# Sorting the tokens by expert inside the attention loop

## The chip, the cores and the metric

One core of a Trainium2 chip runs the whole program. The metric is the device time of one execution in microseconds: the median of three runs. Engines are named as the profile does: PE (matrix products; PEld is its weight loading), DVE (VectorE), ACT (ScalarE), POOL (GpSimd) and SP (SyncE, which issues most transfers).

## What is computed

A cross-attention layer and a mixture of experts, each with a residual:

```python
x = x + xattn(layernorm(x), ctx_1024, cos, sin, ...)      # 8 batches, 512 x 256 rows, 1024 context rows, 16 heads of 64
y = layernorm(x)                                          # the experts' input
shared = gelu(y @ shared_up) @ shared_down                # 256 -> 1024 -> 256
probs = softmax(y @ router_w)                             # 8 experts
top_k_prob, top_k_idx = top_k(probs, 2)
routed = sum(gate[e] * (gelu(y @ routed_up[e]) @ routed_down[e]) for e in the two chosen)
out = x + shared + routed + y
```

The attention's logits are clipped to -11..11 after scaling; all data are float32.

## The kernel before

**Stages.** `prepare` brings in weights and the first batch. `attention` has a loop over seven batches and the eighth one unrolled (`batches`, L543); each batch has eight turns, one for each pair of heads (`slot(b, p)` of every engine, p = 0 to 7, called the first to the eighth turn here). `experts` computes the shared expert for seven batches, then 12 big routed tiles of 512 rows and 15 small ones of 256, and last the shared expert of the eighth batch. Every engine has its program written out in order; semaphores alone tie them together.

**A batch in attention.** In the fifth turn of pass b the attention result of batch b - 1 is normalized: VectorE computes moments, GpSimd the reciprocal root (`rstd`, L693, a power), VectorE `norm_shift` (L1296), ScalarE `normalize` (L1114) from x_out to xn. In the seventh and eighth turns PE transposes xn, and at the end of the eighth computes the router's logits (`route_by_columns`, L865), which ScalarE copies out (`copy_logits`, L1120). SyncE stores xn to `normed` in HBM in the sixth turn (`store_norm`, L558).

**Order in the fifth turn.** GpSimd: the two subtractions of the staged context (`low_stage`, L697), then rstd. VectorE: clip, sums, `multiply_out`, the moments, clips and sums again, then in this order

```python
            clip(4)
            if p == NORMS - 1 or p < NORMS and not last(b):
                norm_shift(p, ...)          # waits for GpSimd's rstd
            add_up(4)
            add_up(5)
```

ScalarE runs the exponentials of scores (L1039) and waits for VectorE's sums before it overwrites one of four probs buffers; at the turn's end it normalizes. PE waits for exponentials (scores) and clips (products with v). SyncE waits for the two subtractions (`store_stage`, L564) before it issues `spread_rden` (L586). In the fourth turn GpSimd has two subtractions of staged x and an rstd. In each turn it also stores a piece of zeros to the sorted rows (L705).

**Routing in the experts.** While the shared expert runs, VectorE takes the logits of all 4096 tokens (32 tiles of 128), finds the two best experts, their gates and the rank of each token among those of its expert (with two matmuls by a triangle and by ones, `rank_rows`), and from the counts the packed start of every expert in units of 256 rows (from L2085 to L2136). Then GpSimd scatters: for each of eight batches it copies four numbers a token beside the row (L1844) and issues eight indirect transfers of 128 rows of 1040 bytes (L1848) to `sorted_rows`, two batches being reloaded to freed buffers on the way (L1853). `s_scatall` then lets SyncE load the first routed rows (L1708). `tables` computes which rows and expert each tile has.

Of the kernel before, what the change touches and what calls it, by code (L numbers as in the profile page):

```python
# [17 lines left out]
P = 128  # L18
ZERO = 325
# [6 lines left out]
class Shapes:  # L26


    def __init__(self, x, ctx, cos, Wq, routed_up):
# [17 lines left out]
        self.DW = self.D + 4  # L47
        assert 2 * self.HD == P and self.KD == 2 and self.N == 512 and self.KT == 8 and self.PAIRS == 8


def prepare(nc, sh, es, mem, x, ctx_in, cos, sin, lat_g, lat_b, ctx_g, ctx_b, Wq, Wkv, Wo, wpack, keep):
# [16 lines left out]
    def sem(name):  # L68
# [8 lines left out]
    AT = dict(k_two=0, k_rope=2048, x_raw=4096, probs=7168, k_two_split=13312, o=15360, o6=18432, x_all=25088, v1=30208,  # L77
              whole=32256, xn_T=33280, den_sb=34304)
# [252 lines left out]
    def scalar_x(act, k):  # L331
# [6 lines left out]
                w_two=w_two, w_five=w_five, k1_two=k1_two, clo=s_clo, lats=s_lats, wvlo=s_wvlo, wout=(s_wout, 48), wo=(s_wo, 16),  # L338
# [3 lines left out]
def attention(nc, sh, es, mem, prep, x, ctx_in, bo, router_w, wpack, ctxT, latT, start, xn_d, xnT, xs, den_d, rden_d, keep):  # L342
# [93 lines left out]
    def result_norm(b):  # L436
# [17 lines left out]
    x_all = sb("x_all", [P, 3, QT, D])  # L454
    x_in, x_out, xn = (x_all[:, i] for i in range(3))
# [9 lines left out]
                 v0=KT * 2 * P, probs=PROBS * 2 * N, k_split=4 * S, o=PAIRS * N, q_all=5 * N, sums=6 * N, x_all=3 * QT * D,  # L465
# [6 lines left out]
    n_var, n_rstd, n_shift = ([sb(f"n_{what}{i}", [P, QT]) for i in range(NORMS)] for what in ("var", "rstd", "shift"))  # L472
    rw = sb("rw", [P, KD, E])
    bo_bc = sb("bo_bc", [P, D])

# [47 lines left out]

    def batches(eng, slot):

        with nc.Fori(0, LAST, engines=[eng.engine], hint_back_edge=True) as b:
            for p in range(PAIRS):
                slot(b, p)
        for p in range(PAIRS):
            slot(LAST, p)  # L530

    def sync(sp, shared_weights, first_rows):
# [19 lines left out]
        sp.sem_inc(s_xnout, 16)  # L552
# [5 lines left out]
        def store_norm(to, n, normed):  # L558
            sp.wait_ge(s_normed, normed)
            sp.dma_start(xn_d[to].rearrange("(p t) d -> p t d", p=P), xn).then_inc(s_xnout, 16)  # L560
# [47 lines left out]
        def slot(b, p):  # L608
# [18 lines left out]
            if p == PAIRS - 3:  # L627
# [5 lines left out]
                store_norm((b + (B - 1)) % B, b + 1, result_norm(b))  # L633
# [36 lines left out]
    def gpsimd(pool):  # L670
        flat = xs.rearrange("r d -> (r d)").rearrange("(c p z) -> c p z", p=P, z=ZERO)
        PARTS = flat.shape[0] // B
        assert PARTS * B == flat.shape[0] and PARTS <= PAIRS
        prep["gpsimd"](pool)
        pool.memset(neg_half[:], -0.5)
        pool.memset(p_sum[1], 1.0)
# [13 lines left out]
        pool.memset(x_out, 0.0).then_inc(s_zeroed, 1)  # L690
# [11 lines left out]

        def slot(b, p):
            if p < PARTS:
                pool.dma_start(flat[b * PARTS + p], keep["zero"][:]).then_inc(s_zero, 16)  # L705
# [6 lines left out]
            elif p < NORMS:  # L712
                rstd(p, b * NORMS + (p + 1))

# [5 lines left out]
        def zeroed():  # L720
            pool.wait_ge(s_zero, 16 * flat.shape[0])
# [3 lines left out]
    def tensor(pe):  # L725
# [150 lines left out]

        def weigh_tile(p, j):
# [6 lines left out]
        def slot(b, p):  # L884
# [44 lines left out]
            def weigh_two(j):  # L929
                pe.wait_ge(s_clip, b * (PAIRS * STEPS) + (G + j + 4))  # L930
                if j == 0:
# [3 lines left out]
                    if p == 0:  # L935
                        pe.wait_ge(s_lgout, b + 1)
                for t in (j, j + 1):
# [49 lines left out]
            if p == PAIRS - 1:  # L987
                pe.wait_ge(s_dencp, b * PAIRS + (p + 2))
                route_by_columns(act_before(b, p, nth(b, p, "t", 1) + 1), sum_ps[:, before_p % 2])
            weigh_two(2)  # L990
# [41 lines left out]
    def scalar(act, split_weights):  # L1032
        act.sem_inc(s_exp, 2)
        act.sem_inc(s_u, 1)
# [85 lines left out]
        def copy_logits(to, n, src):  # L1120
            act.wait_ge(s_lg, n)
            act.activation(logits[:, bass.ds(to * QT, QT)], src[:, 0:QT * E].rearrange("p (t e) -> p t e", e=E),
# [5 lines left out]
        def slot(b, p):  # L1128
# [63 lines left out]
            if p == PAIRS - 1:  # L1192
                copy_logits((b + (B - 1)) % B, b + 1, sum_ps[:, before_p % 2])
# [5 lines left out]
            exps(6, 7)  # L1199
            if p == NORMS - 1 or p < NORMS and not last(b):  # L1200
                if p == NORMS - 1:

                    act.wait_ge(s_xnout, 16 * b + 16)
# [17 lines left out]
        def last_norm():  # L1221
            act.wait_ge(s_xnout, 16 * B + 16)
# [8 lines left out]
        def last_logits():  # L1231
            copy_logits(LAST, B + 1, proj[0])
# [1115 lines left out]
```

## Time and profile before

| | us |
|---|---|
| three runs | 2253.99, 2255.81, 2255.84 |
| median | 2255.81 |
| span of the profiled execution | 2252.6 |

Of the profiled execution the span is what is recorded; the median of the runs is 3.2 us above it. Busy in this execution: PE 2166.5 us (96%), VectorE 1763.5 (78%), ScalarE 1354.5 (60%), GpSimd 419.1 (19%). A busy PE isn't PE at its peak, since ends of matmuls are modelled; an instruction's duration holds the time in which it is held up once it is started. "Issue" as releaser means that the profile shows nothing the engine waited for.

### The profile page before, as it was taken

How to read it: one execution, taken by the hardware profiler on the slowest of the kernel's cores; microseconds unless marked ns; L12 is line 12 of the kernel's file. 1: busy time of each engine (PE TensorE's matmuls, PEld its weight loads, DVE VectorE, ACT ScalarE, POOL GpSimd, SP SyncE). 2: the span in 40 equal slices, each digit the busy share in tenths (PEclk: the TensorE clock that was granted, in tenths of full speed). 3: DMA queues.
4: the chain of work that ended last, by engine and by line, in shares of the span. 5: the costliest groups of instructions: out<-in, count | busy, mean ns of one | idle time of the engine just before them, and what ended most of it. 6: DMA issues, size and time to landing. Idle time of an engine off the chain costs nothing. (4 is left out here: it accounts for less than half of the span.)

```text
span 2252.6 us, 48833 instructions
## 1 busy us (share of the span) xinstructions
PE 2166.5 (96%) x18002; PEld 1591.0 (71%) x18002; DVE 1763.5 (78%) x2342; ACT 1354.5 (60%) x1942; POOL 419.1 (19%) x358
## 2 busy tenths in 40 slices
PE   6999999999999999999999999999639999999999
PEld 5666666666666666666666666648539999999998
DVE  7999899889889899998988988995303565556775
ACT  6675676666567567666656755654114556556775
POOL 2110120111011011011101110004740122223222
PEclk9999999999999999999999999999659999999999
DMA  7344335335334533523533442244542454546773
GB/s 263 91 130 148 89 111 179 89 98 168 107 96 130 154 83 116 177 86 103 171 96 101 147 140 67 59 136 137 195 160 85 136 135 122 140 126 168 224 225 99
DMA packets 154291, 297.77 MB, mean 132 GB/s; under 512 B 34688, under 2 KB 79616, under 8 KB 152064
## 3 DMA queue, kind: packets, MB, share of 16 engines
q1 hardware_dynamic: 136176, 264.60, 38.2%
q0 software_dynamic: 17664, 30.45, 5.8%
q8 instruction: 136, 2.23, 0.4%
q10 hardware_dynamic: 288, 0.26, 0.0%
q14 instruction: 27, 0.22, 0.0%
HBM read 181.44 MB, written 79.72 MB: 116 GB/s over the span
## 5 line engine op out<-in xcount | busy, mean ns | idle before, releaser
L1039 ACT ACTIVATE probs<-scores 128x1024 f32<-128x1024 f32 x512 | 503.6, 1025 | 325.6 <-PE scores L754 312.8
L1345 DVE TENSOR_TENSOR sums<-sums,probs 128x1024 f32<-128x1024 f32 x384 | 470.2, 1225 | 14.2 <-issue 1.7
L880 PE MATMUL sum_ps<-probs,v_nat 128*64 128x512 f32 x2056 | 476.6, 599 | 3.6 <-DVE probs L1244 3.6
L754 PE MATMUL scores<-q_split,k_split 64*128 64x512 f32 x3072 | 415.2, 394 | 1.8 <-ACT probs L1039 1.8
L1244 DVE TENSOR_SCALAR probs<-probs 128x2048 f32<-128x2048 f32 x256 | 314.2, 1227 | 107.8 <-ACT probs L1039 107.4
L1927 PE MATMUL sum_ps<-down,hid_split 128*128 128x256 f32 x2640 | 361.4, 285 | 35.2 <-issue 34.1
L1927 PEld LDWEIGHTS sum_ps<-down,hid_split 128*128 128x128 f32 x2640 | 346.8, 193 | 54.9 <-issue 41.6
L1901 PE MATMUL scores<-xT,up 128*128 128x512 f32 (+1 forms) x1680 | 354.4, 351 | 19.0 <-issue 18.2
L2065 DVE TENSOR_TENSOR hid_split<-hid,hid_split 128x512 fp32r<-128x512 f32 x204 | 141.3, 692 | 252.4 <-ACT hid_split L1991 187.4
L754 PEld LDWEIGHTS scores<-q_split,k_split 64*128 64x128 f32 x3072 | 283.7, 185 | 55.1 <-ACT probs L1039 5.9
L1990 ACT ACTIVATE hid<-scores 128x512 f32<-128x512 f32 x220 | 131.5, 598 | 315.9 <-PE scores L1901 231.8
L1901 PEld LDWEIGHTS scores<-xT,up 128*128 128x128 f32 x1680 | 264.1, 192 | 53.0 <-issue 24.8
L880 PEld LDWEIGHTS sum_ps<-probs,v_nat 128*64 128x64 f32 x2056 | 135.4, 136 | 230.5 <-issue 199.6
L814 PEld LDWEIGHTS proj<-wv,ctx_all 64*128 64x128 f32 x2976 | 189.5, 186 | 31.0 <-issue 19.8
L1869 POOL DMA_INDIRECT out<-y_sb,dest x78 | 128.4, 1647 | 438.4 <-ACT y_sb L2043 399.3
L800 PE MATMUL proj<-ctx_all,w_all 64*128 64x512 f32 x1488 | 198.3, 397 | 6.1 <-DMA ctx_all<-ctx_parts 2.7
L814 PE MATMUL proj<-wv,ctx_all 64*128 64x256 f32 x2976 | 203.9, 283 | 0.0
L800 PEld LDWEIGHTS proj<-ctx_all,w_all 64*128 64x128 f32 x1488 | 142.0, 184 | 76.0 <-issue 45.4
L701 POOL TENSOR_TENSOR stage<-whole,stage 128x512 fp32r<-128x512 f32 x42 | 56.8, 1353 | 524.8 <-ACT stage L1112 524.8
L695 POOL TENSOR_TENSOR n_rstd<-n_var,a_neg_half 128x4 f32<-128x4 f32 x37 | 78.5, 2121 | 285.1 <-DVE n_var L1294 285.1
L1991 ACT ACTIVATE hid_split<-scores 128x512 fp32r<-128x512 f32 x220 | 130.3, 592 | 0.0
L777 PE MATMUL proj<-wo,o 128*64 128x256 f32 x1024 | 115.9, 379 | 0.0
(229 smaller groups left out, 2284.4 us busy)
## 6 DMA issues: line engine op xcount, KB each, us to landing
k_two<-k_two SPq DMA_DIRECT2D x252, 128.0 KB, 2.3
w_all<-wpack SPq DMA_DIRECT2D x60, 512.0 KB, 4.2
raw<-L_ffn_routed_up SPq DMA_DIRECT2D x27, 1024.0 KB
raw<-L_ffn_routed_down SPq DMA_DIRECT2D x27, 1024.0 KB
rden<-rden_rows SPq DMA_DIRECT2D x128, 128.0 KB, 2.9
ctx_parts<-stage SPq DMA_DIRECT2D x28, 512.0 KB, 4.0
ctx_all<-ctx_parts SPq DMA_DIRECT2D x14, 1024.0 KB, 6.5
sorted_rows<-zero POOLq DMA_DIRECT2D x64, 162.5 KB, 2.5
```

The lines of the kernel that those rows point to most:

```text
L754: last = pe.matmul(scores[j % 2][:, head], k_split[i][own, a, j * P:(j + 1) * P], q_split[i][own, m], start=n == 0, stop=n == 2)
L800: last = pe.matmul(proj[to], w[i][halves(g), 0, a, k], ctxs[to][halves(g), m, k], start=phase == 0 and n == 0, stop=phase == 1 and n == 3 ...
L814: last = pe.matmul(proj[to][:, 256 * t:256 * t + 256], ctxs[part][halves(g), a, k, tile], wv[halves(g), duo, m, k], start=phase == 0 and t ...
L880: last = pe.matmul(sum_ps[64 * head:64 * head + 64, p % 2], v_nat[p // 2 % 2][:, j, cols:cols + 64], probs[:, j % PROBS, head], start=j == ...
L1039: act.activation(probs[:, j % PROBS], scores[j % 2][:], ACT.Exp, scale=float(HD) ** -0.5).then_inc(s_exp, 1)
L1244: v.tensor_scalar(pr, pr, EXP_LO, EXP_HI, ALU.max, ALU.min).then_inc(s_clip, 2)
L1345: v.tensor_tensor(to, to, probs[:, j % PROBS], ALU.add).then_inc(s_add, 1)
L1901: last = pe.matmul(to, up[t.wu][:, wp, k * F + g * P:k * F + (g + 1) * P], xT[t.u][:, xp, k, 0:U if t.half else N], start=n == 0, stop=n = ...
L1927: last = pe.matmul(yp[:, q], hs[:, hpart, at:at + P], down[t.wu][:, wp, g * D:(g + 1) * D], start=g == 0 and n == 0 and q % 2 == 0, stop=g ...
L1990: act.activation(hid[f % 2][:], hp[f % 4], ACT.Gelu)
L1991: act.activation(hid_split[f % 4][:, 0], hp[f % 4], ACT.Gelu).then_inc(s_hhi, 1)
L2065: v.tensor_tensor(hid_split[f % 4][:, 1], hid[f % 2][:], hid_split[f % 4][:, 0].bitcast(F32), ALU.subtract).then_inc(s_hlo, 1)
```

## The change

The sorted copy gets one region for each expert, 17 units of 256 rows, in place of packed units, so that a token's place doesn't depend on the counts of all batches. The choice of experts and the scatter of batches 0 to 5 are done in attention, one pass after the logits (passes 2 to 7; passes 0 and 1 do the same work on rows that aren't valid yet and are overwritten); batches 6 and 7 are done in the experts as before.

- VectorE: `first_choice` (5 instructions) at the end of the first turn, `second_choice` (7) at the end of the second, all on 128 x 32 elements or fewer.
- PE: `rank_by_columns`, four matmuls of 32 columns in the third turn; ScalarE: a copy of their result and one exponential of 128 x 36 in the third turn.
- GpSimd: at the end of its fourth turn `route_scatter`, 29 steps, each of which waits for its own completion, and three more instructions; then the scatters of tiles 0 and 1 (four indirect transfers), and first of all in the fifth turn those of tiles 2 and 3 (four more).
- ScalarE's normalize in the fifth turn waits for the eight scatters of this pass (`s_rscat`) in place of the store of xn.
- xn lies in rows of 260 numbers, of which the last four hold token, expert and gates. It is stored to `normed` for batches 6 and 7 alone. The zero stores in attention go; 8 stores of 256 rows of zeros behind each expert's last row are issued by SyncE ahead of the first row loads, and waited for.
- In the experts, routing works on 8 tiles of tokens in place of 32, 16 indirect transfers stand in place of 64, and the reloads go. The packed starts (u_at from counts) become fixed ones.

The core of the diff:

```diff
+        def then(b, ins):
+            step[0] += 1
+            ins.then_inc(s_rstep, 1)
+            pool.wait_ge(s_rstep, b * ROUTE_STEPS + step[0])
+            pool.sem_inc(s_rpass, 1)
+        def over_experts(b, dst, src):
+            then(b, pool.tensor_tensor(r_half[:], src[:, :, 0:4], src[:, :, 4:8], ALU.add))
+            then(b, pool.tensor_tensor(r_half[:, :, 0:2], r_half[:, :, 0:2], r_half[:, :, 2:4], ALU.add))
+            then(b, pool.tensor_tensor(dst, r_half[:, :, 0], r_half[:, :, 1], ALU.add))
+        def route_scatter(b):
+            step[0] = 0
+            then(b, pool.tensor_scalar(r_tok, r_tok, float(N), None, ALU.add))
+            then(b, pool.tensor_scalar(r_valid, r_tok[:, 0:1], 1.0, None, ALU.is_ge))
+            pool.wait_ge(s_rexp, b + 2)
+            over_experts(b, r_tot, r_less[:, :, 0:E])
+            then(b, pool.tensor_tensor(r_gate[0], r_tot, r_neg_one, ALU.pow))
+            then(b, pool.tensor_tensor(r_gate[1], r_less[:, :, E], r_gate[0], ALU.mult))
+            pool.tensor_copy(xn_rows[:, :, D], r_tok)
+            pool.tensor_scalar(xn_rows[:, :, D + 1], r_best[0], float(E), None, ALU.add)
+            pool.tensor_copy(xn_rows[:, :, D + 2], r_gate[1])
+            then(b, pool.tensor_tensor(xn_rows[:, :, D + 3], r_gate[0], r_gate[1], ALU.subtract))
+            pool.wait_ge(s_rrank, b + 1)
+            for t in range(QT):
+                then(b, pool.tensor_tensor(r_pos[:, t], r_rank[:, 0, t], r_next[:], ALU.add))
+                then(b, pool.tensor_tensor(r_next[:], r_rank[:, 1, t], r_next[:], ALU.add))
+            then(b, pool.tensor_tensor(r_next[:], r_next[:], region[:], ALU.subtract))
+            then(b, pool.tensor_scalar(r_next[:], r_next[:], r_valid, None, ALU.mult))
+            then(b, pool.tensor_tensor(r_next[:], r_next[:], region[:], ALU.add))
+            for n in range(2):
+                then(b, pool.tensor_tensor(r_tmp[:], r_sel[n][:], r_pos[:], ALU.mult))
+                over_experts(b, r_posf, r_tmp)
+                then(b, pool.tensor_copy(r_idx[n], r_posf))
+        def scatter_tiles(tiles):
+            for t in tiles:
+                for n in range(2):
+                    pool.indirect_dma_start(xs, ..., xn_rows[:, t], None).then_inc(s_rscat, 16)
         def slot(b, p):
-            if p < PARTS:
-                pool.dma_start(flat[b * PARTS + p], keep["zero"][:]).then_inc(s_zero, 16)
+            if p == 4:
+                scatter_tiles((2, 3))
             for i, (at, kind, k) in enumerate(plan(b, p)):
                 if kind in "cxt":
                     low_stage(...)
@@
             elif p < NORMS:
                 rstd(p, b * NORMS + (p + 1))
+            if p == 3:
+                route_scatter(b)
+                scatter_tiles((0, 1))
@@ ScalarE, the fifth turn
-                    act.wait_ge(s_xnout, 16 * b + 16)
+                    act.wait_ge(s_rscat, SCATTERED * b + SCATTERED)
@@ ScalarE, the third turn
+            if p == 2:
+                act.wait_ge(s_rmax, b + 1)
+                act.activation(r_less[:], r_less[:], ACT.Exp).then_inc(s_rexp, 1)
@@ VectorE, at the end of a turn
+            if p == 0:
+                first_choice(b)
+            if p == 1:
+                second_choice(b)
@@ SyncE in the experts
         sp.wait_ge(s_scatall, 1)
+        for e in range(E):
+            at = sp.value_load(pad_at[0:1, e:e + 1], min_val=0, max_val=(SPARE - 1) * U)
+            sp.dma_start(xs[bass.ds(at, U)]..., keep["zero"][:]...).then_inc(s_pad, 16)
+        sp.wait_ge(s_pad, 16 * E)
@@ GpSimd in the experts
-        for b in range(B):
+        for i in range(2):
```

## Rows read from the trace of the kernel before

**Rows 1.** The page: busy tenths in forty slices of the span; PEclk likewise.

```profile
PE   6999999999999999999999999999639999999999
...
PEclk9999999999999999999999999999659999999999
```

**Rows 2.** Windows: length; busy us (count) of PE, PEld, DVE, ACT, POOL; PEclk, DMA share, GB/s.

```profile
155.00:1527.00 1372.00, 1361.89 (x12329) 882.57 (x12326) 1242.36 (x1453) 873.51 (x1128) 169.40 (x148) 1.00 0.40 119
...
1594.70:1676.00 81.30, 27.73 (x74) 18.36 (x73) 7.28 (x20) 6.25 (x12) 56.09 (x63) 0.52 0.56 189
...
1676.00:1680.80 4.80, 4.78 (x19) 4.38 (x20) 1.07 (x2) 0.26 (x1) 0.00 (x0) 0.57 0.01 3
...
1680.80:2252.60 571.80, 567.34 (x4009) 531.09 (x4007) 341.72 (x567) 341.30 (x606) 128.44 (x78) 1.00 0.52 144
```

**Rows 3.** Timeline (start us, us, engine, line, operation), PE before and in the hole.

```profile
1592.11 1.60 PE L1927 MATMUL sum_ps<-down,hid_split 128*128 128x256 f32 x12
...
1594.93 0.51 PE L1927 MATMUL sum_ps<-down,hid_split 128*128 128x256 f32 x3
...
1638.16 0.29 PEld L1927 LDWEIGHTS sum_ps<-down,hid_split 128*128 128x128 f32 x1 [2.54 <-issue]
...
1639.56 0.37 PE L1927 MATMUL sum_ps<-down,hid_split 128*128 128x256 f32 x1 [2.46 <-issue]
```

**Rows 4.** Waits of PE over the span: us in total, times, longest us.

```profile
PE sum_ps L1927 <- issue: 34.1, 24, 3.1
...
PE scores L1901 <- issue: 18.2, 11, 2.9
```

**Rows 5.** The scatters' line: duration min/median/max ns, first and last start us.

```profile
L1848 POOL DMA_INDIRECT sorted_rows<-rows,idx x32: 959/963/1353, 1582.5 to 1666.1; - x32
```

**Rows 6.** Windows of one batch: fourth turn, fifth turn, sum of the eight turns.

```profile
1053.00:1075.00 22.00, 21.97 (x204) 13.88 (x200) 20.07 (x20) 17.63 (x25) 4.56 (x4) 1.00 0.38 117
...
1075.00:1098.00 23.00, 22.79 (x210) 14.67 (x210) 22.62 (x32) 17.18 (x23) 4.36 (x4) 1.00 0.45 137
...
sum 186.10, PE 185.38 PEld 121.55 DVE 169.21 ACT 120.81 POOL 25.38; mean PE 23.17 PEld 15.19 DVE 21.15 ACT 15.10 POOL 3.17
```

**Rows 7.** Timeline of VectorE and GpSimd, end of fourth turn to n_shift of the fifth.

```profile
864.23 0.68 DVE L1356 TENSOR_TENSOR o<-sums,rden 128x512 f32<-128x512 f32 x1
...
869.09 1.79 POOL L695 TENSOR_TENSOR n_rstd<-n_var,a_neg_half 128x4 f32<-128x4 f32 x1
...
869.62 1.23 DVE L1244 TENSOR_SCALAR probs<-probs 128x2048 f32<-128x2048 f32 x1 [1.64 <-ACT probs L1039]
...
870.10 0.88 POOL L705 DMA_DIRECT2D sorted_rows<-zero  x1
...
870.88 2.49 DVE L1345 TENSOR_TENSOR sums<-sums,probs 128x1024 f32<-128x1024 f32 x2
...
887.16 1.32 POOL L701 TENSOR_TENSOR stage<-whole,stage 128x512 fp32r<-128x512 f32 x1 [16.18 <-ACT stage L1112]
...
887.26 1.77 DVE L1356 TENSOR_TENSOR o<-sums,rden 128x512 f32<-128x512 f32 x1
...
896.80 1.22 DVE L1244 TENSOR_SCALAR probs<-probs 128x2048 f32<-128x2048 f32 x1
...
897.94 0.16 DVE L1298 SCALAR_TENSOR_TENSOR n_shift<-n_mv,n_rstd 128x4 f32<-128x4 f32 x1
```

**Rows 8.** n_rstd's tile view (durations min/median/max ns), and a small copy's timeline row.

```profile
L695 POOL TENSOR_TENSOR n_rstd<-n_var,a_neg_half x37: 1033/2232/2282, 54.5 to 1542.0; 128x4 f32<-128x4 f32 x37
...
1592.76 0.21 POOL L1844 COPY rows<-meta 128x16 f32<-128x16 f32 x1
```

**Rows 9.** Timeline of ScalarE and PE where the sixth turn begins.

```profile
900.05 2.07 ACT L1117 ACTIVATE x_all<-x_all,n_shift,n_rstd 128x256 f32<-128x256 f32 x4
...
903.01 1.95 ACT L1039 ACTIVATE probs<-scores 128x1024 f32<-128x1024 f32 x2 [0.90 <-PE scores L754]
...
904.85 1.52 PE L754 MATMUL scores<-q_split,k_split 64*128 64x512 f32 x12
```

More of the change, by code:

```diff
@@ L18 @@
 P = 128
-ZERO = 325
 EPS = 1e-5
@@ L471, in attention @@
     n_mv = [sb(f"n_mv{i}", [P, QT, 2]) for i in range(NORMS)]
[L472 removed]
+    n_all = [sb(f"n_{what}", [P, NORMS, QT]) for what in ("var", "rstd", "shift")]
+    n_var, n_rstd, n_shift = ([t[:, i] for i in range(NORMS)] for t in n_all)
     rw = sb("rw", [P, KD, E])
     bo_bc = sb("bo_bc", [P, D])
+    tri, region = keep["tri"], keep["region"]
+    lg = logits[:, 0:QT]
+    r_pos, r_tmp, r_both = (sb(f"r_{n}", [P, QT, E]) for n in ("pos", "tmp", "both"))
+    r_below = r_both
+    r_less = sb("r_less", [P, QT, E + 1])
+    r_sel = [sb(f"r_sel{n}", [P, QT, E]) for n in range(2)]
+    r_rank = sb("r_rank", [P, 2, QT, E])
+    r_few = sb("r_few", [P, 10, QT])
+    r_mx, r_tot, r_posf, r_neg_one, r_tok = (r_few[:, i] for i in range(5))
+    r_gate, r_best = ([r_few[:, 5 + 2 * i + n] for n in range(2)] for i in range(2))
+    r_half = sb("r_half", [P, QT, E // 2])
+    r_both_idx = sb("r_idx", [P, 2, QT], I32)
+    r_idx = [r_both_idx[:, n] for n in range(2)]
+    r_next, r_valid = sb("r_next", [P, E]), r_few[:, 9, 0:1]
     scores = [ps(f"scores{i}", [P, 2, N]) for i in range(2)]
@@ L875, in route_by_columns, with rank_by_columns @@
             last.then_inc(s_lg, 1)
+        def rank_by_columns(to):
+            chosen = r_both[:].rearrange("p t e -> p (t e)")
+            for c in range(2):
+                for n, m in enumerate((tri[:, halves(c)], ones[:, 0:64])):
+                    last = pe.matmul(to[halves(c), QT * E * n:QT * E * (n + 1)], m, chosen, start=n == 0, stop=True, skip_group_check=True)
+            last.then_inc(s_rps, 1)
         def weigh_tile(p, j):
@@ L1559, in routing @@
         return ap.rearrange("p (a b) -> p a b", b=shape[1])
-    stage = [t[:] for t in rows] + [t[:, h * QT * DW:(h + 1) * QT * DW].rearrange("p (t d) -> p t d", d=DW)
-                                    for t in pair for h in range(2)]
-    STAGES = len(stage)
-    tri, all_ones, ones_e = routing([P], 1), routing([P], 1), routing([E * NT], 1)
+    stage = [t[:] for t in rows]
+    all_ones, ones_e = routing([P], 1), routing([E * NT], 1)
     unit_steps, two_steps = routing([E, KU], 1), routing([E, KU // 2], 1)
```

199 lines of the change are left out of this document (130 added, 69 removed).

## Prediction

> **What bounds the kernel now.** I read four views in this order: the forty slices of the page, the windows by stage, the waits of PE, and the timeline where PE is not full. The slices show PE at nine tenths or more except at the start and in two slices near 1600 us, where PEclk falls too [rows 1]. The windows give sizes [rows 2]: in attention (155 to 1527 us) PE is busy 1361.9 of 1372.0 us, in the experts after 1680.8 us 567.3 of 571.8. Between them lies a hole of 81.3 us, from 1594.7 to 1676.0, in which PE ran 74 matmuls. The timeline gives what these cost when nothing is wrong: 18 matmuls, one step of a shared tile, take 2.82 us (12 begin at 1592.11, the next 12 at 1594.93) [rows 3]. So 74 are 11.6 us of work, and 69.7 us are lost. In the hole a weight load is followed 1.40 us later by one matmul, and nothing the profile knows is waited for: "issue" [rows 3, 4]. The hole coincides with GpSimd's stream of 64 indirect scatters, first at 1582.5 and last at 1666.1 us, 0.96 us each [rows 5], with 0.3 us between. PE begins to starve 12 us, ten scatters, into the stream and is released about 6 us after its end. After it come 4.8 us at granted clock 0.57 with 19 matmuls, 3.0 us of work: 1.8 us more. The prize is 69.7 + 1.8 = 71.5 us.
>
> The rest is bound by PE: a time in attention counts only where it delays PE. Two turns of a batch show how little room VectorE has: 20.1 busy us of 22.0 in the fourth turn, 22.6 of 23.0 in the fifth, with PE full in both [rows 6].
>
> **The change part by part.** (1) Tail. Of 64 scatters 16 stay (two batches), the reloads go, and the routing chain works on 8 tiles in place of 32. The stream shrinks from 85 us to 16 x 1.27 = 20.3 us. By the trace, 12 us pass before PE feels it and 6 us after; the loss could be 0 (the instructions that PE lacked at 1594.7 come in time) to 20.3 + 6 - 12 = 14 us. I take 5: the shorter chain starts the stream earlier, so it ends near the moment at which PE ran dry. Added on SyncE, past one store and ahead of the first rows: eight stores of zeros with a wait. They are 2.1 MB beside shared tiles that still last over 20 us, and I cost them at nothing; were they uncovered, the first routed tile would wait some 11 us (2.1 MB at the 189 GB/s of the hole [rows 2]). Tail: -71.5 + 5 = -66.
>
> (2) Removed in attention: 64 zero stores and six of eight stores of xn, all hidden. Nothing. PE: four small matmuls a batch; ScalarE: one copy of 64 columns and one exponential of 36, each under the 0.52 us that 256 columns of normalize take [rows 9]: 0 to 1 us a batch. VectorE: 12 tiny instructions, five at the end of the first turn and seven at the end of the second; n_shift, as small, takes 0.16 us [rows 7], so 2 to 3 us a batch, where [rows 6] leave 0.4 to 1.9 us a turn. I take 1 us a batch for both, 8 in all, with ends 0 and 20.
>
> (3) GpSimd in the fourth and fifth turns; this decides. After its rstd of the fourth turn (ends 870.88 in the batch I read [rows 7]) GpSimd now runs `route_scatter`, 32 dependent small instructions, then eight scatters back to back: nothing stands between the two groups of four in its order, so the turns of their name don't spread them. Queued behind them are the two `low_stage` of the fifth turn and its rstd. Who waits for that: VectorE's n_shift, which starts at 897.94 [rows 7], with all of VectorE behind it (the sums that free probs); SyncE's stores of the stage, with spread_rden behind; ScalarE's normalize of x_out, and behind it the exponentials of the sixth turn.
> The budget: rstd alone needs 1.03 us and with the port taken 2.23 [rows 8]; the two subtractions 1.3 us each [rows 7]. For rstd to end by 897.94, the scatters must be done by about 892.7: 22 us from 870.88. Eight scatters take 8 x 1.27 = 10.2 of them, so the 32 instructions have 11.6 us, 0.36 us each.
> What does one cost? With VectorE idle, a copy of 16 columns takes 0.21 us [rows 8] and the power 1.03, so with 0.1 us to the next 32 x 0.31 + 0.8 = 10.7 us: it just fits. But VectorE isn't idle. The rows show one of the two holding the other out for a whole instruction: `o` takes 1.77 us where GpSimd's subtraction began 0.10 us ahead of it, and 0.68 us without; a power that began at 869.09 ends at 870.88 in place of 870.12, with the clip that ran from 869.62 to 870.85 [rows 7]; the median power is 2.23 us against 1.03 at the least [rows 8]. When GpSimd waits at the end of a VectorE instruction it goes next (the subtraction at 887.16 ahead of `o`), and after it VectorE. So one small step per VectorE instruction. From 870.88 to n_shift, VectorE runs 21 large ones, the sums at 870.88 first and the clip at 896.80 last [rows 7], and 3 tiny ones: 24 steps. In the 2.0 us of batch-norm instructions of one operand some 6 more fit. That is 30 of 32 when VectorE reaches n_shift, itself later by 30 insertions of 0.2 us less what its gaps absorb: about 902. Then, with VectorE stopped: 2 steps 0.6, eight scatters 10.2, two subtractions 3.0 with their gaps, rstd 1.2: 917. n_shift moves from 898 to 917, 19 us.
> What PE feels: in the trace the exponentials of the next turn start at 903.01, the scores that need them at 904.85 [rows 9]. With n_shift at 917 normalize (2.07 us [rows 9]) ends at 919.4, the first exponential at 920.4, and the scores follow: 15.6 us later than 904.85. The clip of the last two tiles is 1 us later than that again. I take 16.5 us a batch. It happens in the seven passes of the loop; in the last batch no staging and no rstd stand ahead in the fourth turn, so GpSimd starts a turn earlier: 2 us. 7 x 16.5 + 2 = 118. The ends: 0 (a step of 0.31 us throughout) and 7 x 25 = 175 (each step 1.4 us, the scatters at 1.6).
> Clock: after the hole PE ran 4.8 us at 0.57 before it was at full speed [rows 2]. A stop of 15 us may bring the lower level again: 0 to 2.4 us a batch; I take 1, 7 in all.
>
> Sum: -66 + 8 + 118 + 7 = +67 on a profiled span of 2252.6 us gives 2319.6; the three runs' median stands 3.2 us above the span (2255.81), so 2322.8. I say 2322.
>
> **A rule weighed.** GpSimd's store of zeros at 870.10 took 0.88 us and ended just behind the clip [rows 7]. The Trainium skill, "SBUF — State Buffer" (section "SBUF: two separate sides"), says that while VectorE runs an instruction in a two-port mode GpSimd cannot write descriptors. By it each scatter may be held by up to one clip. Where VectorE stands still for n_shift, as I forecast, the rule costs nothing; were VectorE running, the clips among its work (one in four or five instructions) could each hold one up for its 1.23 us, some 3 us in all, and the forecast would be 7 x 3 = 21 us more. The row at 870.10 agrees with the rule, but it is one row.
>
> **The rivals.** *GpSimd fits (the other sign).* If several small steps pass in each gap, or a step doesn't need the port, 32 steps take 11 to 14 us and n_shift waits 0 to 3 us. For it: 10.7 + 10.2 lies under 22. Against: the median power of the trace was held for 1.2 us [rows 8]. Time: 2255.8 - 66 + 8 + 7 x (0 to 2) = 2198 to 2212. It decides from 58 / 7 = 8 us a batch: below that the change gains.
> *Half way.* Steps held about every second time: 5 to 10 us a batch, 2233 to 2268.
> *The stream starves PE in attention as well.* 64 scatters cost 71 us where they stood in one stream, 1.1 us each. In bursts of eight over 10 us, shorter than the 12 us after which PE starved, I expect none; and the experts' GpSimd adds rows to the result four transfers at a time beside a full PE [rows 2]. If it came and overlapped half with the stop of PE, 56 x 1.1 / 2 = 31 us: 2353; with the upper end of (3), 2380. The Trainium skill, "Runtime: NRT & Kernel Launch" (section "Instruction fetch mechanics"), has PE's instructions fetched ahead by a DMA queue of its own, its cost mostly hidden; the single matmuls every 2.8 us with no releaser don't agree with "hidden".
> *It doesn't do what it says:* the hole stays with 16 scatters, loss 14 to 20 us in place of 5: 2331 to 2337, inside the forecast's range.
>
> **How the numbers follow.** Forecast (VectorE stopped 12 to 22 us a batch, 2285 to 2350): 0.56. GpSimd fits, 2198 to 2212: 0.20. Half way, 2233 to 2268: 0.12, of which half faster, a quarter about the same, a quarter slower. Starved as well, 2350 to 2390: 0.12. Range 2200 to 2358: it leaves out a few hundredths below and most of the last case. Forecast's own range 2285 to 2350. Differences under 0.2% (4.5 us) can't be told from none. Faster by more: 0.20 + 0.06 = 0.26; same 0.03; slower 0.56 + 0.12 + 0.03 = 0.71.
>
> **What would show it.** Right: the wait of VectorE's n_shift on GpSimd's rstd grows from nothing to 10 to 20 us, once a batch in the fifth turn, and ScalarE and PE stand with it; small GpSimd instructions in `route_scatter` start 1.2 to 1.5 us apart while VectorE runs and 0.3 us apart when it stops; the batch, 186.1 us now [rows 6], grows to about 203; the hole at 1600 us shrinks to under 15 us with some 16 scatters in it. Wrong: steps under 0.5 us apart beside a busy VectorE, n_shift on time, a batch of 186 to 188 us. PE showing "issue" in attention would speak for the starved case. The hole staying at 40 us or more would make part (1) wrong.

## The result and the profile after

The changed kernel takes 2321.7 us (median of four runs, 2319.04 to 2324.47) beside 2254.9 us for the kernel before on the same chip (2252.72 to 2255.84): a ratio of 1.0298, with a 95% interval of 1.0283 to 1.0313. It is 3% slower. The profiled execution spans 2319.3 us, 66.7 us more than the 2252.6 before.

Where these 66.7 us lie can be read from GpSimd's last `rstd` of attention, which stands ahead of the experts' tail in both kernels: it starts at 1670.7 us where it started at 1542.0 [rows 8]. Attention and what is ahead of it have grown by 128.7 us, and from there to the end the time fell from 710.6 to 648.6 us, by 62.0.

The page shows the same without a number: the hole near 1600 us [rows 1] has shrunk to a digit, and in its place PE has dents in every batch, with the granted clock dented beside them.

```profile
PE   6988997998899799989979998999989999999999
...
PEclk9999998999899899989989998999999999999999
```

The waits over the span (us in total, times, longest) name the chain that makes the dents: VectorE's `n_shift` stands for GpSimd's `n_rstd`, ScalarE's normalize for `n_shift`, PE's scores for ScalarE's exponentials. The long ones come once a batch, 12 to 17 us at the longest. In the kernel before, `n_shift` waited once, 1.1 us, and PE's scores 1.8 us in all.

```profile
DVE n_shift L1409 <- POOL n_rstd L734: 118.2, 8, 16.9
...
ACT x_all L1222 <- DVE n_shift L1409: 98.7, 7, 14.2
...
PE scores L843 <- ACT probs L1144: 87.6, 12, 12.4
...
PE sum_ps L2073 <- issue: 5.0, 5, 1.7
```

The timeline of one batch (start us, us, then engine, line and operation) shows what GpSimd does meanwhile. This stretch answers to rows 7.

```profile
944.86 1.81 POOL L734 TENSOR_TENSOR n_rstd<-n_var,a_neg_half 128x4 f32<-128x4 f32 x1
945.85 0.87 POOL L759 TENSOR_SCALAR r_few<-r_few 128x4 f32<-128x4 f32 x1
...
950.54 0.96 POOL L755 TENSOR_TENSOR r_few<-r_half 128x4 f32<-128x4 f32 x1 [0.18 <-POOL r_half L754]
...
964.40 0.20 POOL L772 TENSOR_TENSOR r_pos<-r_rank,r_next 128x8 f32<-128x8 f32 x1 [0.18 <-POOL r_next L773]
...
972.15 0.96 POOL L755 TENSOR_TENSOR r_few<-r_half 128x4 f32<-128x4 f32 x1 [0.18 <-POOL r_half L754]
...
974.85 0.20 POOL L755 TENSOR_TENSOR r_few<-r_half 128x4 f32<-128x4 f32 x1 [0.18 <-POOL r_half L754]
...
976.24 1.11 POOL L786 DMA_INDIRECT sorted_rows<-x_all,r_idx  x1 [0.83 <-POOL r_idx L780]
...
985.24 0.96 POOL L786 DMA_INDIRECT sorted_rows<-x_all,r_idx  x1 [0.30 <-issue]
986.21 2.49 POOL L740 TENSOR_TENSOR stage<-whole,stage 128x512 fp32r<-128x512 f32 x2
988.65 1.06 POOL L734 TENSOR_TENSOR n_rstd<-n_var,a_neg_half 128x4 f32<-128x4 f32 x1
```

```profile
963.71 1.39 DVE L1397 BATCH_NORM_STATS2 n_stats<-x_all 128x6 f32<-128x256 f32 x4
...
971.84 1.22 DVE L1355 TENSOR_SCALAR probs<-probs 128x2048 f32<-128x2048 f32 x1
...
989.74 0.16 DVE L1409 SCALAR_TENSOR_TENSOR n_shift<-n_mv,n_rstd 128x4 f32<-128x4 f32 x1 [16.69 <-POOL n_rstd L734]
```

The instruction of line 755 adds 2 x 4 numbers a partition. Beside a VectorE at work it takes 0.96 us, twice; at 974.85 VectorE has stood still since 973.06, and the same instruction takes 0.20 us. Not every VectorE instruction holds it up: beside the moments (the `BATCH_NORM` instructions, 963.71 to 965.52 us) four steps of 8 columns took 0.20 us each. While VectorE runs its other instructions the additions of lines 753 to 755 start 1.14 to 1.22 us apart, once it stands still 0.37 to 0.40. The 32 small instructions run from 945.85 to 975.41 us, the eight scatters to 986.20, then come the two subtractions and the `rstd` for which VectorE waits. Before, `n_shift` stood 27.06 us behind the end of the `rstd` of the fourth turn (897.94 - 870.88 [rows 7]); here it is 989.74 - 946.67 = 43.07 us, 16.0 later.

The windows (as in rows 2 and 6) run from GpSimd's third-turn `rstd` to its fourth, from there to its fifth with the stop in it, and then give the stop and what follows it:

```profile
917.70:944.90 27.20, 27.16 (x270) 18.32 (x270) 22.77 (x31) 18.16 (x26) 4.90 (x4) 1.00 0.35 93
944.90:988.60 43.70, 35.84 (x334) 23.63 (x330) 27.06 (x34) 23.80 (x32) 35.46 (x43) 0.95 0.26 80
...
973.00:989.80 16.80, 7.77 (x52) 4.16 (x48) 0.11 (x2) 2.90 (x4) 12.68 (x18) 0.83 0.23 83
989.80:1003.00 13.20, 8.54 (x42) 3.52 (x42) 12.97 (x14) 8.41 (x12) 0.00 (x0) 0.70 0.68 218
```

VectorE is busy 0.11 of 16.8 us, PE 7.77, and PE's granted clock goes down to 0.83 and 0.70, a mix of 1.2 and 2.4 GHz. PE's busy time over the whole batch says what the clock costs: 187.45 us here for the same 1708 matmuls that take 185.71 us at full clock in the first run below.

```profile
666.80:870.40 203.60, 187.45 (x1708) 121.23 (x1704) 171.58 (x218) 121.00 (x160) 53.54 (x53) 0.97 0.36 107
```

The batch takes 203.6 us (from one first-turn `rstd` to the next, 666.8 to 870.4 us) where it took 186.1 [rows 6]: 17.5 us, seven times, are 122.5 of the 128.7.

In the tail, 16 scatters start at 1707.48 us and end at 1727.81. PE still runs dry, 12.8 us into them, for a short while:

```profile
1720.27 0.48 PE L2047 MATMUL scores<-xT,up 128*128 128x512 f32 x1 [0.30 <-issue]
```

```profile
1720.00:1730.00 10.00, 4.38 (x15) 2.99 (x15) 0.41 (x3) 0.00 (x0) 5.99 (x7) 0.74 0.26 93
1730.00:1740.00 10.00, 9.86 (x49) 8.75 (x48) 7.35 (x24) 4.67 (x9) 0.00 (x0) 0.75 0.21 71
...
1748.00:2319.30 571.30, 567.33 (x4009) 531.11 (x4007) 341.51 (x567) 341.00 (x606) 128.45 (x78) 1.00 0.54 153
```

By the measure of [rows 3], 18 matmuls in 2.82 us, the 64 matmuls of these 20 us are 10.0 us of work: 10 us are lost where it was 71.5. The rest of the experts is as before, 571.3 us beside 571.8 [rows 2].

### The profile page after: what moved, and what is told of

It reads as the page before. It is cut to its first block and busy times, and to the rows that moved or that the text cites. A ratio compares the mean times of both kernels' runs of the same rounds, so it can differ in the third digit from the quotient of the medians.

```text
span 2319.3 us, 49719 instructions
## 1 busy us (share of the span) xinstructions
PE 2175.6 (94%) x18066; PEld 1588.3 (68%) x18066; DVE 1776.2 (77%) x2439; ACT 1355.5 (58%) x1958; POOL 593.1 (26%) x565
## 3 DMA queue, kind: packets, MB, share of 16 engines
q8 instruction: 136, 2.23, 0.4%
## 5 line engine op out<-in xcount | busy, mean ns | idle before, releaser
L843 PE MATMUL scores<-q_split,k_split 64*128 64x512 f32 x3072 | 425.6, 402 | 87.6 <-ACT probs L1144 87.6
L977 PE MATMUL sum_ps<-probs,v_nat 128*64 128x512 f32 x2056 | 482.6, 605 | 12.0 <-DVE probs L1355 11.6
L2073 PE MATMUL sum_ps<-down,hid_split 128*128 128x256 f32 x2640 | 354.5, 284 | 5.2 <-issue 5.0
L2047 PE MATMUL scores<-xT,up 128*128 128x512 f32 (+1 forms) x1680 | 348.8, 349 | 0.7 <-issue 0.5
L740 POOL TENSOR_TENSOR stage<-xn_T,stage 128x512 fp32r<-128x512 f32 x16 | 32.3, 2018 | 433.4 <-ACT stage L1212 433.4
L734 POOL TENSOR_TENSOR n_rstd<-n_var,a_neg_half 128x4 f32<-128x4 f32 x37 | 69.4, 1876 | 183.3 <-DVE n_var L1405 183.3
```

Source lines behind the costliest of these rows:

```text
L843: last = pe.matmul(scores[j % 2][:, head], k_split[i][own, a, j * P:(j + 1) * P], q_split[i][own, m], start=n == 0, stop=n == 2)
L977: last = pe.matmul(sum_ps[64 * head:64 * head + 64, p % 2], v_nat[p // 2 % 2][:, j, cols:cols + 64], probs[:, j % PROBS, head], start=j == ...
L2047: last = pe.matmul(to, up[t.wu][:, wp, k * F + g * P:k * F + (g + 1) * P], xT[t.u][:, xp, k, 0:U if t.half else N], start=n == 0, stop=n = ...
L2073: last = pe.matmul(yp[:, q], hs[:, hpart, at:at + P], down[t.wu][:, wp, g * D:(g + 1) * D], start=g == 0 and n == 0 and q % 2 == 0, stop=g ...
```

## The experiments

Two questions: which part of the new work makes `n_shift` late, and what starves PE beside a stream of scatters. "Before" stands for a run of the kernel before on the same chip; it spread more in these (2239 to 2257 us) than in the first comparison, and a ratio's interval is given with each run.

### Without the small instructions

```diff
             if p == 3:
-                route_scatter(b)
                 scatter_tiles((0, 1))
```

> The changed kernel without the 32 small GpSimd instructions of a batch: the eight scatters of a batch stay where they are, but write always the same 1024 rows at the end of the last region, by a table made once before the loop; the first 768 rows of each region are filled with zeros by one plain transfer a turn, so the experts work on zeros for six batches and the output lacks their part. My theory (the small instructions hold up the three subtractions and the rstd behind them, and so n_shift): VectorE's n_shift waits 0 to 15 us in all for GpSimd's rstd instead of 118, the batch period falls from 203.6 to 186 to 189 us, the time is 2200 to 2225 us. Rival (the eight scatters, as instructions and as traffic, are the cost): the period stays at 193 us or more and the time at 2250 us or more.

Measured 2204.1 us, 117.6 under the changed kernel; 0.979 of before (0.976 to 0.982). `n_shift` waits once, 1.1 us, as in the kernel before; the batch, in a window from one first-turn `rstd` to the next, is 187.9 us with PE at full clock:

```profile
806.00:993.90 187.90, 185.71 (x1708) 121.17 (x1704) 172.66 (x218) 121.01 (x160) 38.54 (x30) 1.00 0.40 122
```

The eight scatters still stand there, beside a busy VectorE, and are dearer than in the tail. The groups of lines (busy us, mean ns of one; here from 160 us on) have them at 1.5 us:

```profile
L787 POOL DMA_INDIRECT sorted_rows<-x_all,r_idx x56 | 84.1, 1502 | 15.2 <-issue 15.2
```

With 0.3 us between them that is 14.4 us a batch on GpSimd, and it costs nothing, since the `rstd` behind them is still on time. The theory holds: the small instructions are needed for the loss.

### Without the scatters

```diff
-                scatter_tiles((0, 1))
...
-            if p == 4:
-                scatter_tiles((2, 3))
```

> The changed kernel with its 32 small instructions a batch, but without the scatters of attention and the waits for them (the regions' first 1536 rows are filled with zeros instead, by six plain transfers a batch; the output lacks the routed part of six batches). Theory: the small instructions alone hold GpSimd some 30 us and the scatters 10, so n_shift is late by 6 to 7 us instead of 17, the period is 192 to 194 us and the time 2240 to 2260 us. Rival (the scatters are the cost): the period is 186 to 189 us, the time 2200 to 2225 us.

Measured 2253.2 us, 68.5 under the changed kernel, 9.8 a batch; 1.001 of before (0.9995 to 1.002). The longest wait of `n_shift` is 7.5 us where it was 16.9:

```profile
DVE n_shift L1410 <- POOL n_rstd L734: 53.3, 8, 7.5
```

Both parts count because they stand in one queue with a due time. The small instructions alone overrun it by 7 us a batch, the scatters alone do not, and both together overrun it by the small ones' 7 and the scatters' 10.

### Small instructions that only write

```diff
-                then(b, pool.tensor_tensor(r_pos[:, t], r_rank[:, 0, t], r_next[:], ALU.add))
+                then(b, pool.memset(r_half[:].rearrange("p t e -> p (t e)")[:, 0:8], 0.0))
```

and so for all 32 (written out here for one), each with its number of elements.

> The changed kernel with each small instruction replaced by one that only writes (a memset of the same number of elements), with the same 29 steps, each of which waits for its own end, and the same 8 scatters (to fixed rows, as in the run without the small instructions; what is left out is the same). Theory (a small instruction takes about 1 us because it reads the memory that VectorE reads too, and gets in between two of VectorE's instructions): a step takes 0.2 to 0.4 us, 32 of them 7 to 13 us, n_shift waits 0 to 20 us in all, and the time is 2200 to 2230 us. Rival (a GpSimd instruction that waits for its own end costs about 1 us in itself): a step stays at 0.9 to 1.1 us, n_shift waits over 100 us in all, and the time is over 2300 us.

Measured 2225.1 us, 96.5 under the changed kernel. The timeline, at the place where the adds took 0.96 us:

```profile
895.79 0.10 POOL L766 MEMSET r_half<- 128x8 f32 x1 [0.15 <-POOL r_half L766]
896.05 0.10 POOL L766 MEMSET r_half<- 128x8 f32 x1 [0.15 <-POOL r_half L766]
...
896.82 1.13 POOL L766 MEMSET r_half<- 128x8 f32 x1 [0.15 <-POOL r_half L766]
```

A step takes 0.10 us and 0.15 us of waiting for its own end; now and then one is held for a VectorE instruction (1.13 us). All 32 take 9.5 us (892.37 to 901.86) in place of 29.6. So waiting for its own end is not what makes a step dear. What the run can't tell is whether it is the reading, or two operands, that gets the real ones held; in the trace of the changed kernel steps with one operand are held as well (a copy of 4 columns at line 767: 1.22 us). It is 21 us slower than the run without small instructions, though `n_shift` waits only 3.9 us in all; its batches are 189.6 to 191.9 us in place of 187.9, and I haven't traced these 2 to 3 us.

### The second four scatters behind the rstd

```diff
-            if p == 4:
-                scatter_tiles((2, 3))
             for i, (at, kind, k) in enumerate(plan(b, p)):
...
             elif p < NORMS:
                 rstd(p, b * NORMS + (p + 1))
+            if p == 4:
+                scatter_tiles((2, 3))
```

> The changed kernel, complete, with the second four scatters moved behind the subtraction and the rstd of GpSimd's fifth turn, so that these no longer queue behind them. The small instructions stay. Theory (whatever stands ahead of rstd on GpSimd delays n_shift one to one): four scatters, 5 us, less ahead of it, so n_shift waits 11 to 12 us a batch instead of 16.9, about 80 us in all, and the time is 2280 to 2295 us. Rival (ScalarE's normalize waits for the same scatters, so nothing is gained): n_shift waits less, but ScalarE's normalize waits for the scatters instead, the period stays at 203 us and the time at 2315 to 2325 us.

Measured 2346.1 us, 24 above the changed kernel. Both theories missed, mine by its sign. `n_shift` does wait 5 us less each time, but normalize, which overwrites the rows, now waits for the scatters that read them:

```profile
DVE n_shift L1409 <- POOL n_rstd L734: 82.9, 8, 11.8
...
ACT x_all L1222 <- DMA sorted_rows<-x_all,r_idx: 138.1, 8, 19.9
```

The four scatters are issued beside a VectorE that has just started again (two of them took 2.05 and 1.96 us) and end at 1008.2 us, while in the changed kernel, at the same point of its batch (the fourth-turn `rstd` at 961.4 and 944.9 us), normalize could start at 989.9 + 16.5 = 1006.4. What is moved out of one wait has to be asked for its own reader.

### The arithmetic on VectorE and TensorE

TensorE sums the ranks over the four tiles with 16 small matmuls a pass in place of 4, so that what is left are 14 VectorE instructions, and GpSimd keeps the eight scatters:

```diff
+        def route(b):
+            v.wait_ge(s_rrank, b + 1)
+            then(b, v.tensor_tensor(r_pos[:], rank, r_next[:].unsqueeze(1).broadcast_to((P, QT, E)), ALU.add))
+            then(b, v.tensor_tensor(r_tb[:], r_sel_all[:], r_pos[:].unsqueeze(1).broadcast_to((P, 2, QT, E)), ALU.mult))
+            then(b, v.tensor_reduce(r_atf[:], r_tb[:], AX.X, ALU.add))
+            v.tensor_copy(r_both_idx[:], r_atf[:])
...
             if p == 3:
-                route_scatter(b)
-                scatter_tiles((0, 1))
+                pool.wait_ge(s_ridx, b + 1)
+                scatter_tiles((0, 1, 2, 3))
```

> The changed kernel, complete, with the arithmetic of the rows' places moved: TensorE sums the ranks over the four tiles itself (15 small matmuls a pass in place of 2), VectorE does what is left in 14 instructions in its fourth turn, and GpSimd only issues the eight scatters, all of them at the end of that turn. Theory: GpSimd has 10 us of scatters and no small instructions, so n_shift is on time (0 to 15 us of waits in all); VectorE's 14 instructions take about 5 us in a stretch where it has slack; the period is 186 to 190 us, the time 2195 to 2225 us, about 1.5 to 2.5 per cent under the kernel before. Rival (VectorE has no slack there, and what GpSimd sheds comes back on it): a period of 191 us or more and 2235 us or more.

Measured 2234.8 us, 0.9925 of before (0.990 to 0.995): 87 us under the changed kernel, and 10 above what I expected. `n_shift` is on time. The batch is 191.3 to 192.8 us, and the window from the fourth-turn `rstd` to the fifth's shows why:

```profile
897.60:922.70 25.10, 24.29 (x238) 15.86 (x236) 24.02 (x43) 18.93 (x26) 15.25 (x12) 1.00 0.43 138
```

VectorE is busy 24.02 of 25.10 us; in the run without small instructions this window was 22.1 us long with 21.19 busy. The rival held: VectorE has no slack in this turn.

### Half of it back on GpSimd, a turn earlier

```diff
             elif p < NORMS:
                 rstd(p, b * NORMS + (p + 1))
+            if p == 2:
+                gates(b)
             if p == 3:
                 pool.wait_ge(s_ridx, b + 1)
```

> The run with the places worked out on VectorE, complete, with the other half of that arithmetic (the gates and the row tags, 11 small instructions) given back to GpSimd, but one turn earlier, at the end of its third turn, where nothing waits behind it. Theory: VectorE was full in the fourth turn (24.0 us busy of 25.1), so nine small instructions less there, 2 us, shorten the batch from 191.8 to 189 or 190 us, and the time from 2235 to 2215 to 2225 us. Rival (each small GpSimd instruction holds VectorE up by as much as its own would cost): the period stays at 191 to 193 us, the time at 2230 to 2240 us.

Measured 2224.8 us, 0.989 of before (0.987 to 0.991); the batch is 190 us. The fourth-turn window is back at 22.8 us with 22.02 busy:

```profile
892.10:914.90 22.80, 22.50 (x212) 14.28 (x211) 22.02 (x34) 17.70 (x25) 15.53 (x13) 1.00 0.51 152
```

Of the eleven small GpSimd instructions of one batch four took 1.04 to 1.21 us and seven 0.19 to 0.73, and nothing that has a due time stands behind them: `n_shift` is on time. That all 32 would cost as little a turn earlier was not tried.

### The tail with a pause

```diff
+            if i == 1:
+                pool.wait_ge(s_scat[0], 16 * 2 * QT)
             for t in range(QT):
                 for n in range(2):
                     pool.indirect_dma_start(xs, ...
```

> The same, complete, and in the tail GpSimd waits until its first eight scatters have landed before it issues the second eight. Theory (the pile of scatters starves PE): PE no longer waits for its instructions in the tail (under 2 us in all), and the time is 2 to 6 us under that of the run without the pause. Rival (16 scatters cost PE nothing any more, or the second eight come late for the first routed tile): the time is within 2 us of it, or 2 to 5 us above.

Measured 2215.4 us, 0.985 of before (0.982 to 0.987), 9.4 us under the run without the pause, more than expected. PE has no "issue" among its waits in the tail any more, where it had 5.7 us without the pause. The same 20 us of both kernels, first without and then with the pause:

```profile
1622.00:1642.00 20.00, 14.00 (x60) 11.07 (x59) 7.71 (x27) 5.18 (x10) 7.64 (x8) 0.74 0.18 58
```

```profile
1622.00:1642.00 20.00, 18.36 (x118) 16.16 (x117) 12.28 (x36) 8.38 (x16) 8.41 (x8) 1.00 0.60 202
```

### The kernel before with a pause after each eight

If a pause helps with 16 scatters, it should help where 64 stood in one stream, with nothing else changed:

```diff
                                             stage[i][:, t], None).then_inc(s_scat[i], 16)
+            pool.wait_ge(s_scat[i], 16 * 2 * QT * (1 + b // STAGES))
```

> The kernel before, complete, with one wait more in its tail: after each eight scatters GpSimd waits until they have landed. Theory (the scatters pile up somewhere on the way, and PE's instructions come late only once the pile is deep: PE ran dry 12 us into the stream in both kernels): with the pile emptied every 10 us PE does not run dry for long, the time lost near 1600 us falls from 70 us to under 25, and the time is 2185 to 2215 us. Rival (the scatters take the fetch of PE's instructions as long as they run, at whatever pace): the stream gets longer by 8 pauses of 2 us and the hole with it, 80 to 95 us are lost, and the time is 2260 to 2280 us.

Measured 2206.6 us beside 2248.8 for before in that comparison: 0.981 (0.978 to 0.984). Repeated beside the next two:

> The kernel before with a pause after each eight scatters, once more beside the finer brake, to compare the two on one chip: 2202 to 2210 us by either theory, since it was 2206.5 us the first time.

Measured 2206.8 us (2205.1 to 2206.9) beside 2253.3: 0.9815 (0.977 to 0.986). The hole is gone; 40 us out of what was the hole [rows 2]:

```profile
1630.00:1650.00 20.00, 20.00 (x129) 17.96 (x128) 6.19 (x10) 7.49 (x14) 13.81 (x16) 1.00 0.57 187
1650.00:1670.00 20.00, 20.00 (x128) 18.02 (x127) 5.52 (x9) 6.52 (x12) 9.86 (x10) 1.00 0.46 164
```

What is left is that the stream gets longer. Its last scatter starts at 1693.1 us where it was 1666.1, and PE runs out of shared tiles at 1683.7:

```profile
PE proj L1942 <- DMA rows<-sorted_rows: 16.2, 1, 16.2
```

The view of the DMA queues, taken by stretches, looks as if it named the cause. One queue, q8, carries instructions in packets of about 16 KB (136 packets, 2.23 MB over the span of before; with 18002 matmuls and as many weight loads that is 62 bytes for each, so I take it for PE's). In the 94 us ahead of the hole, 1500 to 1594 us of before, it moved five packets (columns: packets, MB, share of 16 engines):

```profile
q8 instruction: 5, 0.08, 0.3%
```

In the hole of the same kernel, 1594 to 1676 us, the view has one instruction queue, another one, and no line for q8:

```profile
q14 instruction: 4, 0.03, 0.1%
```

In the same stretch of the kernel with the pauses q8 moves its packets again:

```profile
q8 instruction: 4, 0.07, 0.3%
q14 instruction: 6, 0.05, 0.2%
```

But these counts do not tell the cause from the effect. The windows of the same two stretches of before have what PE ran in them:

```profile
1500.00:1594.00 94.00, 93.00 (x608) 73.97 (x607) 61.16 (x108) 44.50 (x73) 35.22 (x40) 1.00 0.46 163
1594.00:1676.00 82.00, 28.43 (x77) 18.92 (x76) 7.28 (x20) 6.25 (x12) 56.49 (x64) 0.53 0.55 187
```

Five packets went with 1215 matmuls and weight loads, 243 for each; the 153 of the hole are less than one packet holds, so a PE that is slow for any reason would move none. The times say the same. The last packet of before moved at 1587 us and the one ahead of it at 1566, 21 us apart, so that none was due at 1594.7, when PE began to run dry. In the changed kernel q8 moved one between 1716 and 1717 us, 4 us before PE ran dry:

```profile
q8 instruction: 1, 0.02, 6.4%
```

So the runs show that PE falls to single matmuls, for which the profile has no releaser, beside an unbroken stream of scatters, and that a wait in GpSimd cures it. The mere load of the transfers is not it: with the pauses the same 82 us move more (215 GB/s in the repeated run, 187 in before) beside a PE that is nearly full. That instructions come late is a guess which these counts do not bear out, and what PE lacks stays open.

### A finer brake, and a coarser one

```diff
+                if b > 0 and t in (0, 2):
+                    pool.wait_ge(s_scat[(b - 1) % STAGES][t // 2], 16 * QT * (1 + (b - 1) // STAGES))
```

> The kernel before, complete, with a finer brake in its tail: GpSimd issues each four scatters once all but the last four have landed, so at most eight are under way, and it need not stand still at the end of each eight. Theory (PE is starved by the number of scatters that are under way, and the pauses only delay the end of the stream): PE is as full as with a pause after each eight, the stream ends some 10 us earlier, and of the 16 us that PE then waited for the first routed rows 5 to 10 go: 2194 to 2204 us. Rival (the pauses themselves let PE's instructions through, and eight under way at all times starve it): the hole comes back in part, 2215 to 2250 us.

Measured 2241.0 us (median of all ten runs, 2218 to 2259), 0.994 of before (0.990 to 0.998). The rival's time held. At most eight scatters were under way, yet GpSimd hardly ever stood still: the last scatter starts 86.1 us after the first, where it was 83.7 in before. PE is dry again, with single matmuls and the granted clock at the lower level:

```profile
1640.00:1650.00 10.00, 5.26 (x16) 3.98 (x15) 0.69 (x1) 1.08 (x2) 7.59 (x10) 0.50 0.27 98
1650.00:1660.00 10.00, 3.88 (x9) 2.58 (x9) 0.00 (x0) 0.00 (x0) 7.58 (x10) 0.50 0.29 103
```

```diff
+            if b % 2 == 1:
+                pool.wait_ge(s_scat[i], 16 * 2 * QT * (1 + b // STAGES))
```

> The kernel before, complete, with the pause only after each 16 scatters, four in all. Theory (PE runs dry some 12 us, ten scatters, into a stream and is free again when the pile is gone): of each 20 us some 5 to 10 are lost, 20 to 40 us in all, and the time is 2205 to 2230 us, PE dry in the second half of each 16. Rival (the pile grows slowly, over many more than 16): nothing is lost, and the time is that with a pause after each eight or a little less, 2195 to 2206 us.

Measured 2197.9 us (2193.9 and 2201.9), 0.978 of before (0.972 to 0.984), the fastest of all. It is 9 us under the pause after each eight, by two runs that lie 8 us apart. PE does run dry at the end of the first and third sixteen, and is full again right behind the pause:

```profile
1600.00:1610.00 10.00, 6.54 (x25) 5.57 (x25) 4.95 (x16) 2.25 (x5) 6.70 (x8) 0.66 0.42 148
1610.00:1620.00 10.00, 10.00 (x67) 8.96 (x66) 3.79 (x6) 4.18 (x8) 8.20 (x9) 1.00 1.01 341
```

From 1594 to 1660 us PE ran 321 matmuls, 50.3 us of work by the measure of [rows 3]: 15.7 us are lost, about as much as the 16 that the pauses after each eight cost at the end.

```profile
1594.00:1660.00 66.00, 57.40 (x321) 49.47 (x321) 17.09 (x34) 19.44 (x36) 45.68 (x49) 0.90 0.63 227
```

So a limit of eight under way is not enough, while a wait until all have landed brings most of the hole back: after 10 us in one kernel, after 20 in the other. Two readings fit this, and no run tells them apart. PE may need the full stop; or it may need only a slower stream, since the last scatter starts 95 us after the first with the pauses after sixteen and 109 with those after eight, against 84 and 86. The same 64 scatters spread evenly over 95 to 109 us were not tried.

## Why the prediction was right

The forecast was 2322 us and the time is 2321.7. The mechanism was right; that the number agrees to 0.3 us is luck, since four terms were each off by 4 to 13 us and cancel.

- **Tail, -66.** Measured -62.0. The 71.5 us of the hole went and 10.0 came back in place of 5: I had the starving begin near the end of the stream, since the stream would start earlier. It began 12.8 us after the first scatter, as in the kernel before (12 us), and lasted past the last one. Stores of zeros and the routing chain cost nothing, as said.
- **Small additions, 8.** The run without small instructions has all else of the change in attention (and one plain store of zeros a turn more): 187.9 us a batch in place of 186.1, so 7 x 1.8 = 12.6.
- **GpSimd, 118.** The mechanism, its chain and its place were right. The stages after the end of the fourth turn's `rstd`: the small instructions end 28.7 us later (I had 902.6 - 870.88 = 31.7), `n_shift` 43.1 us later (46.1), so it is 16.0 us late and not 19. The failing step is that I had VectorE held up by 30 insertions and arrive at 31 us; it arrived at 26.4 (973.06 - 946.67), with 26 steps done. It lost nothing by them that the trace shows. On the other side I let PE feel 2.5 us less than VectorE; PE's batch grew by 17.5 - 1.8 = 15.7 us for a delay of 16.0.
- **Clock, 7.** PE's granted clock was 0.83 and 0.70 in and behind the stop. PE's busy time for the 1708 matmuls of a batch grew by 187.45 - 185.71 = 1.7 us, 12 in all, where I had 1 us a batch. The other 14.0 of the 15.7 are idle time, so the clock is within the 15.7 and not beside it as in my sum. Clock and wait together: 7 x 15.7 = 110 in place of 7 x (16.5 + 1) = 122.5.
- **The rest** of the 128.7 us, 6, lies in the start and the first pass of the loop (3.6: the start is 0.8 us later, and the first pass grew by 2.8 more than the others) and in the last batch (2.4; I had said 2).

The sum: -62.0 + 12.6 + 110 + 6 = +66.6. Mine was -66 + 8 + 118 + 7 = +67. The 12.5 us too much for the stop of VectorE were met by 4 too little for the tail, 5 for the small additions and 4 for the ends of the loop.

The rivals. *GpSimd fits* gave 2198 to 2212 us; the run without small instructions gives 2204.1. The nearer test of this rival is the run with write-only steps, whose 32 steps take 9.5 us with `n_shift` on time but for 3.9 us: it took 2225.1, 13 us above the rival's range, so its price is not shown right. *Half way* (2233 to 2268) is what the run without the scatters shows by its size: `n_shift` late by up to 7.5 us, 2253.2 us, though there every step was as slow as in the changed kernel. *The stream starves PE in attention as well:* it does not; PE has no wait for "issue" in attention in the changed kernel, with bursts of 10 us and a pause of 190 between. *It doesn't do what it says* has some truth in the tail: a loss of 10 us lies between the 5 of the forecast and the 14 to 20 of that rival.

The rule weighed, the Trainium skill's "SBUF — State Buffer" (section "SBUF: two separate sides"), says that GpSimd cannot write descriptors while VectorE runs in a two-port mode. As forecast it cost nothing here: VectorE stood still while the scatters were issued, at 0.96 us each but for the first (1.11). Where VectorE is at work, as in the run without small instructions, a scatter takes 1.50 us in the mean, which agrees with the rule: 0.54 x 8 = 4.3 us a batch, in a place where they are hidden. It isn't the clips alone that hold a scatter: those at 887.38 and 893.53 us of that run took 1.68 us each beside `sums` and no clip, which my 3 us left out. The other page named, "Runtime: NRT & Kernel Launch" (section "Instruction fetch mechanics"), has the cost of fetching instructions mostly hidden. I had held PE's single matmuls against it; since the packets of q8 follow from what PE ran, no run here shows that the fetch was late, and none speaks against the page.

## What to carry to other kernels

Here a small dependent instruction on GpSimd had about the price of one VectorE instruction (0.96 us) beside most of VectorE's work, five times what it took alone: count steps, not elements, and ask what has a due time behind them in GpSimd's queue before asking what they compute. A long unbroken run of indirect DMAs went with a full PE falling to single instructions with no releaser, about 12 us after its start; when a trace shows this, try a wait of the issuing engine for its transfers every ten to twenty us. An instruction queue that is silent in that stretch proves nothing until its packets are set against the instructions that the engine ran. Here that one wait (2198 or 2207 us) brought more than the whole restructuring at its best (2215 us), so the cheap cure of a hole is to be tried before work is moved out of it.

## What the runs showed of the hardware that I had not expected

- VectorE did not pay for the small GpSimd instructions put in between its own: it reached its wait 26.4 us behind the mark beside 26 of them, and 27.1 with none before (with its gaps then).
- A step that only writes took 0.10 us beside a busy VectorE, with 0.15 us to the next; one that reads took 0.96 beside clips and sums and 0.20 beside the moments.
- With at most eight indirect scatters under way but hardly a stop PE runs dry; with sixteen in one go and a stop it loses far less (0.994 against 0.978 of before).
- The hole of the kernel before is not of one length: its runs spread from 2239 to 2257 us in one comparison, and with the pause from 2205 to 2207.
- GpSimd's scalar operation of line 766, a constant added to 4 columns, took 2.32 us in the median of its eight, more than twice a plain step; the one of line 775, whose scalar comes from memory, took 1.38 us.
